# A three-layer graph filter and a selective-scan block on one core: four TensorE hop matmuls and one state sum moved, and ten of GpSimd's C products done in pairs

## The reference, cut to what matters

```python
h = layernorm(x)
e = leaky_relu(sj[:, None, :] + si[:, :, None] + ab)          # sj, si from h @ Wv + bv
t = adj * exp(e);  t = t / sum(t, -1)
H = 0;  Xk = h
for k in range(3):
    H = H + Xk @ Wk[k] + bk[k]
    Xk = t @ Xk
x = x + relu(H)
```

```python
u, z = split(layernorm(x) @ W_fc1.T @ W_in.T);  u = silu(conv4(u))
dt, B, C = split(u @ W_xproj.T);  delta = softplus(dt @ W_dt.T + b_dt)
for each time t:  h = exp(delta_t * A) * h + (delta_t * u_t) * B_t     # 1024 channels x 16 states
                  y_t = sum over the 16 states of h * C_t
x = x + (y + u * D) * silu(z) @ W_out.T @ W_fc2.T
```

## Time and profile before

| | us |
|---|---|
| three runs | 3736.74 (median), 3719.45, 3741.27 |
| the profiled execution, whole | 3739.78 |
| its span, first to last instruction | 3738.0 |
| VectorE busy | 3521.1 (94%) |
| TensorE busy | 3471.2 (93%) |
| GpSimd busy | 3411.8 (91%) |
| ScalarE busy | 2962.9 (79%) |
| TensorE's mean granted clock | 0.98 of full speed |

### The profile page before, as it was taken

One profiled execution on the slowest core, in us unless ns is written; L12 is line 12 of the kernel. 1 busy time (PEld: TensorE's weight loads), 2 busy tenths in 40 slices (PEclk: granted clock), 3 DMA queues, 4 the chain that ended last, 5 costly groups with the idle time before them and its releaser, 6 DMA issues.

```text
span 3738.0 us, 43683 instructions
## 1 busy us (share of the span) xinstructions
PE 3471.2 (93%) x11130; PEld 1965.5 (53%) x11130; DVE 3521.1 (94%) x2877; ACT 2962.9 (79%) x6578; POOL 3411.8 (91%) x1703
## 2 busy tenths in 40 slices
PE   5899999999999999999999999999999999999887
PEld 3555555555555555555555555555555555555433
DVE  0499999999999999999999999999999999999998
ACT  2588788888878888888888788788878888887874
POOL 0399999999999999999999999999999999999998
PEclk9899999999999999999999999999999999999999
DMA  3111101111100111110111110111110111110110
GB/s 112 53 56 59 59 12 49 56 58 58 58 22 40 56 58 58 58 47 15 58 55 58 59 55 12 53 56 58 58 58 9 53 55 58 58 54 9 46 51 9
DMA packets 50720, 183.68 MB, mean 49 GB/s; under 512 B 7356, under 2 KB 33220, under 8 KB 42086
## 3 DMA queue, kind: packets, MB, share of 16 engines
q1 hardware_dynamic: 48898, 174.17, 12.1%
q10 hardware_dynamic: 1636, 7.83, 0.5%
HBM read 164.15 MB, written 17.83 MB: 49 GB/s over the span
## 4 chain that ended last, share of the span: by engine, by line
POOL 44%; issue 26%; PE 14%; ACT 8%; DVE 7%; POOLq 1%; DMA 0%; ACTq 0%; DVEq 0%; SPq 0%
POOL st L425 30%; POOL st L416 8%; PE y_ps L773 5%; DVE st L967 4%; ACT dec L491 3%; POOL delta L398 3%; POOL du_sb L406 2%; DVE st L955 2%; PE d_ps L810 2%; PE d_ps L830 1%; PE g L926 1%; POOL rstd L383 1%; PE d_ps L852 1%; ACT L491 1%; DVE u L992 1%
## 5 line engine op out<-in xcount | busy, mean ns | idle before, releaser
L425 POOL TENSOR_TENSOR st<-st,bc 128x1024 f32<-128x1024 f32 x1024 | 2404.9, 2364 | 162.3 <-DVE st L967 161.9
L967 DVE TENSOR_TENSOR_SCAN st<-dec,st 128x1024 f32<-128x1024 f32 x1024 | 2316.3, 2279 | 11.7 <-ACT dec L491 5.1
L773 PE MATMUL y_ps<-st,ident 128*128 128x512 f32 x4096 | 1928.1, 605 | 130.1 <-POOL st L425 129.0
L491 ACT ACTIVATE dec<-delta,decay 128x254 f32<-128x254 f32 x4096 | 1691.7, 464 | 309.7 <-DVE st L967 307.5
L773 PEld LDWEIGHTS y_ps<-st,ident 128*128 128x128 f32 x4096 | 751.1, 192 | 957.4 <-issue 654.3
L955 DVE TENSOR_TENSOR st<-du,bc 128x1024 f32<-128x1024 f32 x736 | 886.4, 1204 | 2.2 <-ACT du L477 2.2
L416 POOL TENSOR_TENSOR st<-du_sb,bc 128x1024 f32<-128x1024 f32 x288 | 680.7, 2364 | 0.1
L539 ACT ACTIVATE u<-d_ps,bconv,chan 128x256 f32<-128x256 f32 x256 | 129.8, 557 | 258.7 <-PE d_ps L810 258.6
L810 PE MATMUL d_ps<-xnT,wxz 128*128 128x256 f32 x1024 | 261.9, 401 | 70.0 <-DVE u L992 69.3
L992 DVE SCALAR_TENSOR_TENSOR u<-d_ps,chan,u 128x250 f32<-128x250 f32 (+2 forms) x768 | 307.1, 474 | 6.1 <-ACT u L539 6.1
L810 PEld LDWEIGHTS d_ps<-xnT,wxz 128*128 128x128 f32 x1024 | 197.3, 198 | 143.6 <-DVE u L992 103.6
(11 more groups left out here) (111 smaller groups left out, 2534.3 us busy)
## 6 DMA issues: line engine op xcount, KB each, us to landing
bc<-bc_dram SPq DMA_DIRECT2D x64, 2048.0 KB, 9.8
xg<-x_dram SPq DMA_DIRECT2D x32, 256.0 KB, 11.5
x_dram<-xg SPq DMA_DIRECT2D x32, 256.0 KB, 2.0
last_x<-x_dram SPq DMA_DIRECT2D x32, 256.0 KB, 2.6
out_dram<-last_x SPq DMA_DIRECT2D x32, 256.0 KB, 2.1
bc<-w_inT_dram ACTq DMA_DIRECT2D x1, 4096.0 KB, 13.9
adjt<-adjT_dram SPq DMA_DIRECT2D x32, 128.0 KB, 11.2
bc<-w_out_dram ACTq DMA_DIRECT2D x1, 2048.0 KB
```

What stands on the lines that cost most here:

```text
L425: nc.gpsimd.tensor_tensor(st[:, sl, :, :, :], st[:, sl, :, :, :], bc[:, p, 1, SU * q:SU * q + SU, None, :].to_broadcast([P, SU, 2, T]), AL ...
L491: a = nc.scalar.activation(dec[:, v % 2, s, j, :].rearrange("p (b t) -> p b t", b=PAIR)[:, :, 1:], delta[:, p, 2 * i + j, :].rearrange("p ...
L773: mm = nc.tensor.matmul(y_all, ident[:, :], st[:, sl, s, :, :].rearrange("p j t -> p (j t)"), start=False, stop=(q == Q - 1 and s == SU - ...
L967: nc.vector.tensor_tensor_scan(h, dec[:, v % 2, :, :, :].rearrange("p s j t -> p (s j t)"), h, 0.0, ALU.mult, ALU.add).then_inc(S["scanned ...
```

## The change

Three things are edited. **(a)** `graph_pe` does both sequences of the last hop at graph step 26 (step 4), so what stood at step 5 now comes ahead of the sums of units 2 and 3. **(b)** At step 8 (`v == Q`) the sum of unit 7 is issued ahead of `project_out`. **(c)** GpSimd multiplies units (2, 3), (4, 5), (8, 9), (16, 17) and (24, 25) by C in one instruction of 128 x 2048, at the step of the second unit, and behind the scan of the second; it adds 2 to `c_times`.

```diff
+C_PAIRS = (2, 4, 8, 16, 24)
@@ gpsimd body
-                        c_product(pool, k, p, v)
+                        if v - 1 in C_PAIRS:
+                            c_product(pool, k, p, v - 1, 2)
+                        elif v not in C_PAIRS:
+                            c_product(pool, k, p, v, 1)
@@ c_product
-                wait(pool, "scanned", U * k + v + 1)
+                wait(pool, "scanned", U * k + v + n)
-                nc.gpsimd.tensor_tensor(st[:, sl, :, :, :], st[:, sl, :, :, :],
-                                        bc[:, p, 1, SU * q:SU * q + SU, None, :].to_broadcast([P, SU, 2, T]),
-                                        ALU.mult).then_inc(S["c_times"], 1)
+                units = st[:, sl:sl + n, :, :, :].rearrange("p w s j t -> p (w s) j t")
+                nc.gpsimd.tensor_tensor(units, units,
+                                        bc[:, p, 1, SU * q:SU * (q + n), None, :].to_broadcast([P, SU * n, 2, T]),
+                                        ALU.mult).then_inc(S["c_times"], n)
@@ tensor body
                     if scan:
+                        if v == Q:
+                            state_sum(pe, k, p, v - 1)
                         if has_previous(k):
                             project_out(pe, k - 1, r, OUT_STEPS.get(v, ()), ends)
...
-                        if v % Q != 1 and v > 0 and v not in (3, 5):
+                        if v % Q != 1 and v > 0 and v not in (3, 5, Q):
                             state_sum(pe, k, p, v - 1)
@@ graph_pe
-                if v in (26, 27):
+                if v == 26:
-                    b = v - 26
                     wait(pe, "x1k_made", g + 1)
-                    if b == 0:
-                        nc.tensor.matmul(g0[:, :], ones3, bk_row, start=True, stop=False, skip_group_check=True)
-                    hop(b, 0, False, False)
-                    mm = nc.tensor.matmul(g0[:, b * DIM:(b + 1) * DIM], att[:, b, :], x1k[:, b, :],
-                                          start=False, stop=(b == PAIR - 1), skip_group_check=True)
-                    if b == 1:
-                        mm.then_inc(S["h_mm"], 1)
+                    nc.tensor.matmul(g0[:, :], ones3, bk_row, start=True, stop=False, skip_group_check=True)
+                    for b in range(PAIR):
+                        hop(b, 0, False, False)
+                        mm = nc.tensor.matmul(g0[:, b * DIM:(b + 1) * DIM], att[:, b, :], x1k[:, b, :],
+                                              start=False, stop=(b == PAIR - 1), skip_group_check=True)
+                    mm.then_inc(S["h_mm"], 1)
```

More of the change, by code:

```diff
@@ L418, in inject, with c_product @@
                                         ALU.mult).then_inc(S["p_injected"], 1)
-            def c_product(pool, k, p, v):
+            def c_product(pool, k, p, v, n):
                 if v == 0:
                     wait(pool, "c_loaded", 16 * k + 16)
-                wait(pool, "scanned", U * k + v + 1)
+                wait(pool, "scanned", U * k + v + n)
                 q, sl = v % Q, v % SLOTS
-                nc.gpsimd.tensor_tensor(st[:, sl, :, :, :], st[:, sl, :, :, :],
-                                        bc[:, p, 1, SU * q:SU * q + SU, None, :].to_broadcast([P, SU, 2, T]),
-                                        ALU.mult).then_inc(S["c_times"], 1)
+                units = st[:, sl:sl + n, :, :, :].rearrange("p w s j t -> p (w s) j t")
+                nc.gpsimd.tensor_tensor(units, units,
+                                        bc[:, p, 1, SU * q:SU * (q + n), None, :].to_broadcast([P, SU * n, 2, T]),
+                                        ALU.mult).then_inc(S["c_times"], n)
             walk(pool, body, lambda pool, k, p: None)
```

## The result

| us | before | with the change |
|---|---|---|
| runs, median | 3726.09 (6 runs, 3719.45 to 3741.27) | 3769.03 (6 runs, 3766.59 to 3772.24) |
| profiled execution, its span | 3738.0 | 3767.3 |
| VectorE busy | 3521.1 | 3530.0 |
| VectorE idle (span less busy) | 216.9 | 237.3 |
| a group, mean from 300 us on | 111.58 | 112.54 |

The ratio is 1.0101, 95% interval 1.0084 to 1.0119. The forecast was 3708. In the profiled executions the change costs 29.3 us: 20.4 us more idle time on VectorE, and 8.9 us more in which it counts as busy, which I put down to instructions behind a wait overlapping less with their neighbours; no run isolates that.

What follows compares the result with a forecast made beforehand. VectorE was taken as the bound, stalled by falls of TensorE's clock. Span 3738.0 - 32 (falls gone) + 5 (sum 7 first) - 2 (last group) = 3709, then + 1.8 - 3.0 gives 3708 us; forecast's own range 3698 to 3720.

Steps and rivals of the forecast that it cites:

- What bounds it: VectorE bounds the kernel; TensorE's clock falls before the last hop, costing VectorE 3.2 us in every third group.
- (a), nothing: Both last hops in step 4: no gain, since after a fall the wait of 3.2 us would move to the taps.
- (b), 0.5 us lost again, +5 us: Sum of unit 7 first: quarter 0's gate wait of 0.5 us goes but returns at quarter 1's gate, plus 0.16 a group.
- (c), pair 2, 4, 8, free: C products of units 2 to 5 and 8, 9 in pairs: no cost, as GpSimd lags the scans or TensorE comes later.
- (c), pair 16, put at nothing: Units 16, 17: TensorE idles about 1.8 us, sums and dt projection end 1.2 us later, no cost in the sum.
- The decays of unit 24, with 0.2 us to spare: Behind ScalarE's copy of the late dt projection, the decays of unit 24 still come 0.2 us before they are needed.
- (c), pair 24, 32 us gained: Units 24, 25: later sums shorten the idle time before the second u projection, ending ten stalls of 3.2 us.
- 2.02 becomes about 1.0: TensorE's idle time before the second u projection shrinks, as 0.9 to 1.2 us of lateness carries into the next group.
- The clock falls elsewhere: Rival: falls at the sums of 16 or 24, 3748 us for one place (chance 0.15), 3788 for both (0.05).
- A reading: TensorE's starts after a semaphore carry some 0.1 us each that may shrink; it spoke for keeping the gate's gain.
- Quarter 1's gate does not wait: Sign that the forecast is wrong; it expected a wait of 0.5 to 0.7 us at that gate.

Runs made afterwards that it cites:

- e10: Kernel before with the last hops one step earlier and the output projection's bias and first block moved from step 8 to 7: 3691.67 us, ratio 0.9895.
- e3: Kernel before with only both last hops done in step 4: 3734.28 us, ratio 1.0006.
- e2: Changed kernel without the pairs 16, 17 and 24, 25, so with pairs 2, 4 and 8 only: 3728.67 us, ratio 0.9998 against the kernel before.
- e4: Kernel before with only the sum of unit 7 issued ahead of the output projection: 3724.28 us, ratio 0.9985.
- e6: Changed kernel without the pair of units 24 and 25: 3746.40 us, ratio 1.0030 against the kernel before.
- e1: Kernel before with only the five pairs of C products, TensorE's order untouched: 3760.75 us, ratio 1.0092.
- e12: e10 with units 16 and 17 multiplied by C in one instruction: 3761.79 us, ratio 1.0091 against the kernel before.
- e5: Changed kernel without the pair of units 16 and 17: 3724.47 us, ratio 0.9969 against the kernel before.
- e11: e5 with the row-scaling matmuls (L907) issued ahead of the last part of the z projection: 3713.88 us, ratio 0.9956 against the kernel before.
- e7: Kernel before with the sum of unit 2 done at step 3 instead of step 4: 3723.00 us, ratio 0.9961.
- e9: Kernel before with the last hops one step earlier, at steps 3 and 4: 3792.64 us, ratio 1.0165.

## Why the prediction was wrong, step by step

- *What bounds it.* Right: VectorE, busy for 998 of 1000 us in e10, and where it waits in the steady part. That the fall of the clock sits behind the waits at the add was right too.
- *(a), nothing.* Right, with the mechanism: e3 moved the wait from L1046 to the taps, 3.27 us for 3.19 behind a fall of 10.2 us.
- *(b), 0.5 us lost again, +5 us.* With the three free pairs the sum was about right, 7 us (e2). Alone it is 15 us, and that e4 comes out even is luck, owed to shorter falls. The place was wrong. I had the gate of quarter 1 wait 0.5 to 0.7 us. It never does. The x projection, in the same gapless stretch of TensorE, is followed by ScalarE's copy, and that by the du copy and the decays of unit 16, which are needed earlier than the gate: up to 0.7 + 0.45 us in e4, 0.35 to 0.45 at the decays and 0.2 at the du copy in the changed kernel. I looked at the end of the stretch and not at those waiting inside it.
- *(c), pair 2, 4, 8, free.* Nothing in e2 speaks against it; it was not measured alone. The time of a pair, 4536 ns by the sum, was right at 4536 in the mean.
- *(c), pair 16, put at nothing.* The failed step. The idle time of 1.8 us was right (1.75 to 2.05 in 19 groups, 2.4 in nine), and that the dt projection would be late. "The decays of unit 24, with 0.2 us to spare" holds where no fall comes: with 1.75 us of idle time and no fall, neither the changed kernel nor e6 has a wait there. It leaves out the fall, and that is what was wrong: I took 1.8 us as safer than 2.0, because idle times of 1.3 to 1.4 were never followed by a fall. Between 1.4 and 2.0 I had no row. In the changed kernel falls follow this idle time in 16 groups, and the decays of units 22 and 24 wait 23.7 us, a term that the sum has at zero. In e6 falls follow 1.75 us in 17 groups of 27, in e1 2.2 to 2.6 in 25, in e12 2.7 in 23. Where the idle time is 2.7 us (e12), lateness costs 0.8 us a group even without a fall.
- *(c), pair 24, 32 us gained.* Half right. Falls at the u projection go from 13 to 2 when this pair is added without pair 16 (e5), and that brings about 4 us, since a part is given back at the loop's edge (11 us in e5, a wait that the sum does not have) and the falls of e2 cost less than the ones in my trace. The step "2.02 becomes about 1.0" was wrong: 1.72 or 2.12 us remain, and 1.5 in e11, where the loop's edge costs nothing. So at most 0.5 us of the 1.5 was carried, not 0.9 to 1.2, and that most falls went all the same was luck. With pair 16 in, nine falls come there again, and the 32 us gained are 20.7.
- *The rivals.* "The clock falls elsewhere", at unit 16, is what happened, at a chance of 0.15. I had it cost 3.2 to 5 us in every third group; it cost 1.0 to 1.5 us (e6) or about 1.8 (e12), in more than half of the groups. That the gain at the u projection would go as well I had not combined with it.
- *A reading.* The 0.1 us that TensorE's starts after a semaphore are said to carry is 0.05 in the trace before (the product of unit 21 ends at 1920.61, its sum starts at 1920.66); nothing in the sum hangs on it.
- *What would show it wrong.* "Quarter 1's gate does not wait" came true; the idle time before the u projection is not near 1.0 us, and groups are not even (110.66 to 114.38).

Of the 29 us between the two profiled executions VectorE's waits give: decays +38.1, loop edge +11.9, taps +11.2, du copy +3.9; residual add -30.4, gate -17.8. That is +16.9 of the 20.4 us of idle time; the rest are small ones. In the sum's own terms, over the 28 steady groups: the falls at the u projection -20.7 for -32 (add -32.0, taps +11.3); (b) +2.3 for +5 (gate -13.2, decays and du copy of unit 16 +15.5); pair 16 +23.7 for 0; the loop's edge +11.9 for 0.

**What stays open.** Why the same idle time is followed by a fall in one group and not in the next, and what makes a fall last 10.2 us, 6.8 or 3.4. The length of the idle time alone does not decide it. At the u projection 2.0 to 2.1 us is followed by a fall in 10 groups of 28 before, in 2 of 13 in e5, in 1 of 28 in e6 and in none of 13 in e1; at the sums 1.75 us in 17 of 27 (e6), 2.6 in 13 of 28 (e7), 2.2 to 2.6 in 25 of 28 (e1). In e6 and e1 falls stand at the sum of unit 16, earlier than the u projection, and that may be what keeps them away from there; but of the ten groups of e6 without one only one has a fall at the u projection, and no run tests it. The Trainium skill (TensorE: Matmul & The Clock Gate, Part 1) has the gate's count run freely. Executions of one kernel whose falls differ agree with that (the 25 of the kernel before beside e1 have a mean granted clock of 0.978 to 0.987 and take 3745.76 to 3708.70 us), and no run here tests it. Whether it is also how busy the stretch around the idle time is can't be told from these kernels, in which both change together.

## What to carry to other kernels

Look for TensorE's longest idle times first, and count every place that an edit lengthens one: merging two instructions of the engine that feeds it, so as to save 0.14 us, held its input back by one instruction, and in the clean kernel that cost 0.8 us a group by lateness and 1.8 more for each fall of the clock. Filling one idle time can move it to the next instruction that waits for the same feeder: of e9 and e10, which differ in one line, only the one with both places filled is free of falls in the steady part. Where an engine is gapless over a stretch, price a delay at every consumer inside the stretch, not at its end. And where a kernel comes out even, compare its groups without a fall: e2 and e4 came out even because shorter falls hid what their edits cost.

## What the runs showed of the hardware that I had not expected

- Falls of TensorE's clock to half followed idle times of 1.75 us as well as of 2.7, and lasted from 3.4 to 10.2 us. In the steady part (to 3450 us) idle times of up to 1.58 us (those before the sum of unit 24, in 28 groups each of four kernels) were followed by none, nor was the one of 1.72 before the second u projection (15 groups each of the changed kernel, e1 and e5).
- A fall of 3.4 us at the second u projection cost VectorE nothing (e4), one of 6.8 us 1.6 (e3), one of 10.2 us 3.2. Behind the sum of unit 16 one of mostly 3.4 us cost 1.8 (e12). Behind the sum of unit 6, on the path of every group, it cost about half its length: 1.7, 3.3 and 4.9 us (e9).
- An injection behind the loop's branch started 0.8 to 1.1 us late in every turn of the loop (13 times, 11 to 12 us) when the last waiting instruction before the branch was released late, and not otherwise (e5 and e11).
- GpSimd's 2048 elements took 4.54 us against 2.36 for 1024, and VectorE's scans in that kernel ran as before (mean 2.275 us for 2.279).
